# Splitting the last layer's weights: two operations per block on ScalarE and VectorE in place of two on ScalarE and four on GpSimd

## What is computed

```python
x = x + tanh(g_xattn[0]) * fp8_product(layernorm(x), ctx)              # stage A
x = x + tanh(g_ffn[0])   * moe_top2_and_shared(layernorm(x), ...)      # stage B, 8 experts, hidden 128
x = x + tanh(g_xattn[1]) * causal_attention(layernorm(x), ctx, ctx)    # stage C, 16 heads, 4 batches
# stage D, 8 experts, hidden 1024, top 2
probs = softmax(gelu(x @ rw1) @ rw2)
wgt, idx = top_k(probs, 2)
for e in range(8):
    Ye = gelu(x @ w1[e] + b1[e]) @ w2[e] + b2[e]
    ...                                                                # added where idx == e, times wgt
```

## Time and profile before

| | us |
|---|---|
| median of 3 runs | 485.41 |
| lowest, highest | 485.38, 487.7 |
| profiled execution | 489.3 |
| its span, first to last instruction | 487.2 |

### The profile page before, as it was taken

How to read it: one execution, slowest core, us unless ns; L and a number is a source line. 1 busy time by engine, 2 the same in 40 slices (tenths; PEclk the granted TensorE clock), 3 DMA queues, 4 the chain that set the end, 5 groups by cost and what they waited for, 6 DMA issues and landing times.

```text
span 487.2 us, 8683 instructions
## 1 busy us (share of the span) xinstructions
PE 340.7 (70%) x2694; PEld 230.5 (47%) x2695; DVE 316.7 (65%) x787; ACT 269.5 (55%) x541; POOL 182.5 (37%) x232
## 2 busy tenths in 40 slices
PE   0052786977949878468596635008699999999991
PEld 0041324753336565255353312006567777777760
DVE  3978675750554756737779446766757878887870
ACT  1711661054853367858766874614337777777760
POOL 3107026323772414625244554410024455444522
PEclk9996697978979988769979755557989999999997
DMA  8700003604355111463813232365447777777731
GB/s 281 292 0 0 2 0 130 67 0 131 86 147 91 43 49 44 133 108 87 110 45 89 75 111 87 89 217 196 187 146 225 225 227 264 259 223 222 221 34 22
DMA packets 27202, 60.48 MB, mean 124 GB/s; under 512 B 4209, under 2 KB 17858, under 8 KB 23970
## 3 DMA queue, kind: packets, MB, share of 16 engines
q1 hardware_dynamic: 21202, 52.67, 34.8%
q0 software_dynamic: 4416, 6.13, 7.7%
q10 hardware_dynamic: 1552, 1.27, 0.9%
HBM read 29.00 MB, written 6.85 MB: 74 GB/s over the span
## 4 chain that ended last, share of the span: by engine, by line
DVE 23%; PE 22%; issue 18%; ACT 16%; DMA 12%; POOL 5%; ACTq 2%; SPq 1%; DVEq 0%; POOLq 0%
PE bank L1134 9%; ACT arena L1004 5%; DMA STG<-in_l_w_dram 4%; DVE arena L2058 3%; DMA W<-in_ctx_t_dram 3%; ACT arena L1011 3%; POOL W L624 3%; DVE arena L2063 3%; DVE MX L1811 2%; DMA arena<-k_parts 1%; DMA W<-k_parts 1%; DVE arena L2068 1%; ACT STG L791 1%; POOL rstd L599 1%; DMA arena<-token_rows,GI 1%
## 5 line engine op out<-in xcount | busy, mean ns | idle before, releaser
L1467 PE MATMUL bank<-arena 128*128 x184 | 63.4, 390 | 0.9 <-DVE arena L2063 0.9
L1004 ACT ACTIVATE arena<-arena,B1D 128x128 f32<-128x128 f32 x184 | 57.2, 391 | 9.3 <-DVE arena L2058 9.2
L624 POOL TENSOR_TENSOR W<-STG,W 128x256 f16<-128x256 f32 x64 | 41.3, 678 | 50.4 <-ACT W L798 50.4
L2058 DVE TENSOR_REDUCE arena<-bank 128x256 f32<-128x512 f32 x92 | 57.1, 679 | 0.3 <-PE bank L1452 0.3
L691 POOL DMA_INDIRECT arena<-token_rows,GI x23 | 22.9, 995 | 77.3 <-ACT WS L998 56.2
L1470 PE MATMUL bank<-arena 128*128 x184 | 51.2, 278 | 0.0
L1134 PE MATMUL bank<-arena 128*128 128x256 f32 x160 | 44.4, 442 | 7.2 <-ACT arena L839 6.3
L624 POOL TENSOR_TENSOR arena<-STG,arena 128x256 f16<-128x256 f32 x56 | 36.7, 687 | 33.3 <-ACT arena L798 33.3
L704 POOL DMA_INDIRECT out_dram<-arena,SI x23 | 37.0, 1609 | 30.5 <-DMA out_dram<-arena,SI 20.2
L2063 DVE SCALAR_TENSOR_TENSOR arena<-arena 128x512 f16<-128x512 f32 x46 | 29.7, 688 | 26.3 <-ACT arena L1011 25.2
L1449 PE MATMUL bank<-arena 128*128 128x256 f16 x256 | 45.6, 278 | 0.9 <-DVE arena L2010 0.7
(11 more groups left out here) (288 smaller groups left out, 760.0 us busy)
## 6 DMA issues: line engine op xcount, KB each, us to landing
STG<-in_l_w_dram SPq DMA_DIRECT2D x32, 512.0 KB, 3.6
arena<-W SPq DMA_DIRECT2D x16, 1024.0 KB
STG<-W SPq DMA_DIRECT2D x7, 1024.0 KB
arena<-in_l_w_dram SPq DMA_DIRECT2D x2, 1280.0 KB, 11.0
k_parts<-W SPq DMA_DIRECT2D x2, 768.0 KB, 4.9
W<-k_parts SPq DMA_DIRECT2D x12, 128.0 KB, 5.9
arena<-k_parts SPq DMA_DIRECT2D x12, 128.0 KB, 5.8
X<-in_x_dram SPq DMA_DIRECT2D x2, 512.0 KB, 5.7
```

The source lines that it names most:

```text
L624: ins = nc.gpsimd.tensor_tensor(l, src, h, ALU.subtract)
L1004: ins = nc.scalar.activation(x, x, ACT.Gelu, bias=B1D[:, e, c:c + 1], scale=1.0 / (X_SCALE * W_SCALE))
L1467: nc.tensor.matmul(bank[6 + q][:, :], GDL[:, q, 0, c * P:(c + 1) * P], W2[:, e, c].rearrange("p s d -> p (s d)"), start=(c == 0), stop=Fal ...
L2058: v.tensor_reduce(half, o, AX.X, ALU.add).then_inc(s_dadd, 1)
```

## The change

ACT writes the high part straight from the raw block, with the factor 64 in the same operation; the buffer stays raw. DVE computes `64 * raw - high` and writes the low part, in one operation of 1024 columns. POOL does nothing for the weights any more. A block's semaphore chain is load, high (ACT), low (DVE), and load i+2 waits for DVE's low i. The orders written out by hand are new: in stage B DVE's low i follows as `LOW_AFTER` says, in the attention rounds each stands behind every second maximum, and ACT's high i takes one step u where scale and high took two. Loads, and SP's stream as a whole, stand in the order they stood in.

```diff
+        LOW_AFTER = {2 * CA - 8: 3, 2 * CA - 6: 4, 2 * CA - 4: 5, 2 * CA - 2: 6, 2 * CA - 1: 7}
...
             sp.wait_ge(s_eid, 1)
-            sp.wait_ge(s_wlo, BLOCKS - 2)
+            sp.wait_ge(s_wlo, MIDDLE + 2)
             for r in range(2):
                 load_tile_weights(r, r, first=True)
-            sp.wait_ge(s_wlate, 2)
+            sp.wait_ge(s_wlo, BLOCKS)
             load_tile_weights(2, 2, first=True)
...
-                nc.scalar.activation(STG[:, i % 2], STG[:, i % 2], ACT.Copy, scale=W_SCALE).then_inc(s_wscaled, 1)
-
-            def weights_high(i):
-
                 _, hi, _ = weight_block(i)
-                act.wait_ge(s_wscaled, i + 1)
                 src = STG[:, i % 2] if len(hi.shape) == 2 else STG[:, i % 2].rearrange("p (c d) -> p c d", d=D)
-                nc.scalar.activation(hi, src, ACT.Copy).then_inc(s_whi, 1)
+                nc.scalar.activation(hi, src, ACT.Copy, scale=W_SCALE).then_inc(s_whi, 1)
...
+            def weights_low(i):
+
+                _, hi, lo = weight_block(i)
+                dve.wait_ge(s_whi, i + 1)
+                src = STG[:, i % 2] if len(hi.shape) == 2 else STG[:, i % 2].rearrange("p (c d) -> p c d", d=D)
+                v.scalar_tensor_tensor(out=lo, in0=src, scalar=W_SCALE, in1=hi,
+                                       op0=ALU.mult, op1=ALU.subtract).then_inc(s_wlo, 1)
...
                 if b + 1 < B:
+                    blocks = list(C_BLOCKS[b])
                     for u in range(12):
                         maximum(b + 1, u)
+                        if blocks and u % 2:
+                            weights_low(blocks.pop(0))
                     minus_maximum(b + 1)
...
+            for i in D_BLOCKS[3:]:
+                weights_low(i)
+
             def rows_t(j, q, first=False):
```

More of the change, by code:

```diff
@@ L615, in _ @@
             ins.then_inc(s_kparts, 1)
[L617 to L625, removed]
             pool.wait_ge(s_w0, 2)
@@ L649, in _ @@
             pool.wait_ge(s_va, 4)
-            for i in range(9, 11):
-                weights_low(i)
             for g in range(2, 4):
@@ L658, in _ @@
                     estimate_rstd(10, 2, 2)
[L659 to L663, removed]
+                if b == B - 2:
+                    for g in range(2):
+                        estimate_rstd(8 + g, g, 2)
                 if b == 0:
@@ L769, in _, with weights_high @@
             store_xq_t(0, bank[0])
-            def weights_scale(i):
+            def weights_high(i):
                 if i == 0:
@@ L863, in _ @@
             for i in range(3):
-                weights_split(i)
+                weights_high(i)
             store_gates_t(1, bank[2])
@@ L942, in _ @@
             for b in range(B):
-                steps = [(f, i) for i in C_BLOCKS[b] for f in (weights_scale, weights_high)]
+                blocks = list(C_BLOCKS[b])
                 for u in range(12):
@@ L957, in _ @@
                         hidden_weight(b + 1)
-                    if steps and u >= SPLIT_FROM[b]:
-                        f, i = steps.pop(0)
-                        f(i)
+                    if blocks and u >= SPLIT_FROM[b]:
+                        weights_high(blocks.pop(0))
                 store_o(b, 1)
@@ L1775, in _ @@
             choose_gates(1, bank[2])
+            weights_low(0)
             add_down(2)
             store_gate_parts(1, bank[3])
+            weights_low(1)
             add_down(3)
+            weights_low(2)
             dve.wait_ge(s_masks, 4)
@@ L1782, in _ @@
                 gate_hidden(n)
+                if n in LOW_AFTER:
+                    weights_low(LOW_AFTER[n])
                 if n == CA + 3:
@@ L1864, in _ @@
                 maximum(0, u)
+                if u == 6:
+                    weights_low(9)
             minus_maximum(0)
+            weights_low(10)
             add_down(6)
@@ L1896, in _ @@
                     scaled_rows(2)
+                    for i in C_BLOCKS[b]:
+                        weights_low(i)
             for i in range(2):
@@ L1911, in _ @@
                                    op0=ALU.mult, op1=ALU.subtract).then_inc(s_rw, 1)
+            for i in D_BLOCKS[:2]:
+                weights_low(i)
             for h in range(2):
@@ L1924, in _ @@
                             ALU.subtract).then_inc(s_dl, 1)
+            weights_low(D_BLOCKS[2])
             dve.wait_ge(s_ex, 1)
@@ L2024, in _ @@
             v.tensor_tensor(COEF[:, :, 2 * E:3 * E], COEF[:, :, 0:E], SLOTQ[:, :, :], ALU.add).then_inc(s_coef, 1)
-            for i in D_BLOCKS[-2:]:
-                _, hi, lo = weight_block(i)
-                dve.wait_ge(s_whi, i + 1)
-                v.tensor_tensor(lo, STG[:, i % 2].rearrange("p (c d) -> p c d", d=D), hi,
-                                ALU.subtract).then_inc(s_wlate, 1)
             def idle_outputs_out():
```

25 lines of the change are left out of this document (7 added, 18 removed).

## The result

| | before | changed |
|---|---|---|
| median, us | 487.03 (20 runs) | 492.44 (20 runs) |
| ratio of the times, 95% interval | | 1.012 (1.0095 to 1.0145) |
| profiled execution | 489.3 | 491.9 |
| its span | 487.2 | 490.1 |

A forecast was written before the change was run, and what follows sets the result against it. No single engine was taken to bound it: the weight ring, DVE's maxima, key stacks, exponentials, router and first gather did. Terms -3.5 + 1.4 + 1.15 + 0.45 - 3.8 + 9.5 = +5.2 on 485.41 gave 490.6 us, range 484.5 to 496.

The forecast's parts named there:

- Term 1: Second half of stage B: a shorter weight ring starts PE's down(4) earlier, -3.5 us (-4.9 if the fill holds nothing).
- Term 2: Maxima of batch 0: low 9 among them delays the start of round 0, +1.4 us (0 to 1.4).
- Term 3: Attention rounds 0 to 2: DVE's low parts partly in line, less a key stack gain, +1.15 us (-3.2 to +10).
- The key stack's share: Round 0: batch 2's key stack, issued sooner by SP, lets PE start earlier, 3.2 us regained.
- Terms 4 and 5: Round 3, ACT's high 24 waits for its load, +0.45 us; then the way to the router's choice, -3.8 us.
- term 5: Way to the router's choice: DVE's small operations quicker without POOL beside them, router product earlier, -3.8 us (-2.4 to -5).
- Term 6: Token rows: late low 29 holds load 31 and the stores behind it, delaying the first gather, +9.5 us (+6.5 to +11.7).
- about 8 us: Sign of being right: the first gather comes about 8 us behind the row numbers.
- The low bound: Token rows at the start of stage D: +6.5 us if the gather lands sooner with less traffic beside it.
- Rival 2: Token rows not held because the stores go out early: -4.1 us in all, 481.3, chance 0.04.
- Rival 1: Rounds 0 to 2 follow ACT, whose relief gives back 11.6 us while low parts hide: -9.4 in all, 476.0, chance 0.10.
- rival 4: Rounds 0 to 2: every low part in line on DVE, 13.4 us, +9.2 more, 499.8, chance 0.06.

The follow-up runs named there:

- b0: The kernel before, run again with no edit: ratio 0.9984 to the kernel before.
- e3: The kernel before with SP's three token-row stores moved ahead of load 31: ratio 1.0012 to the kernel before.
- a0: The changed kernel, run again with no edit: ratio 1.0133 to the kernel before.
- e1: The changed kernel with DVE's low 29 moved early, right behind the tokens' expert weights: 478.57 us, ratio 0.986 to the kernel before.
- e2: The changed kernel with SP's three token-row stores moved ahead of load 31, DVE's order untouched: 482.08 us, ratio 0.9899 to the kernel before.
- f0: e1 repeated: 479.78 us, ratio 0.9899 to the kernel before.
- f3: f2 with low 9 moved from among batch 0's maxima to behind its negated maximum: 470.67 us, ratio 0.968 to the kernel before.
- e6: The changed kernel with GpSimd's fill held back until DVE's first maximum of batch 0: 493.41 us, ratio 1.0111 to the kernel before.
- e4: The changed kernel with low parts of blocks 11 to 21 (attention rounds 0 to 2) replaced by fp16 copies: ratio 0.9964 to the kernel before.
- e5: The changed kernel with ACT's old two operations for the eleven blocks of rounds 0 to 2: 497.07 us, ratio 1.0198 to the kernel before.
- f1: e1 with the weight work of rounds 0 to 2 (blocks 11 to 21) put back to the old way: 476.69 us, ratio 0.9842 to the kernel before.
- f2: e1 with the first low part of each of rounds 0 to 2 moved into DVE's waits: 473.82 us, ratio 0.9791 to the kernel before.

## Why the prediction was right, term by term

The sum was +5.2 and the time came out at +5.4. That the path was right (a gain ahead of the row numbers, a larger loss behind them) was foresight; that the two figures differ by only 0.2 was in part luck, since the terms below missed by 0.7 to 2 us each, and as measured add up to +2.9. The terms, against the means of the table (three traces of the old order; the changed order's, where a stretch has no further edit):

| term | forecast | measured |
|---|---|---|
| 1, 2: up to max 0 | -2.1 | -3.4 |
| 3: rounds 0 to 2 | +1.15 | +2.3 |
| 4, 5: max 3 to GI | -3.35 | -5.4 |
| 6: GI to the first sums | +9.5 | +10.2 |
| loop | 0 | -0.8 |

**Term 1** was right in mechanism and 0.7 short: down(4) came 4.2 us earlier after the tanh gap, not 3.5, though the fill held DVE as walked. The one difference from the walk that I see is the clock: the first eighteen up products took 4.04 us, not 5.73. The granted clock in their first 4 us was 0.55 to 0.60 in the kernel before and 1.00 in the changed one; b0 and e3 show it lowered there too, and a0, e1, e2, f0 and f3 at 1.00. e6 tested the fill: without the hold down(4) came 1.1 earlier, where I had put 1.4 (4.9 against 3.5). **Term 2**: low 9 was in line, +0.8 from down(4) to max 0; what it may cost through the clock was in no row I had.

**Term 3** had its shape right. Max 0 to 1 grew by 5.6 us (5.4 forecast), max 1 to 2 shrank by 5. Of the 5.6, 1.0 in the mean lies ahead of round 0 (a0, e2 and f0, where the clock fell behind low 9), which I had not priced. The step that failed is how much of a low part reaches the round's end, and what ACT's relief gives: I put a third and nearly nothing; e4 and e5 showed six to nine tenths (8 to 12 us for eleven blocks) and 3 to 8 back. The errors nearly cancelled. The key stack's share was measured by no run alone. SP did issue it sooner, as I had walked, 4.1 to 4.5 us behind max 1 in place of 10.0 to 12.1. But the check I had named, PE waiting less for the keys of batch 2, came out wrong: it waited 5.10 us against 4.62, and 2.5 to 6.0 in the five traces of the changed order against 3.7 to 5.6 in the three of the old. The stretch did shrink, from max 1 to PE's first score 14.3 us against 20.8, but PE reached that point earlier too.

**Terms 4 and 5** were 2 short, nearly all of it in term 5: from max 3 to DVE's first denominator of round 3's output there were 0.2 us less in the mean (+0.45 forecast), from there to GI 5.3 less (-3.8). DVE's four refinement steps took 0.16 each (0.6 in the earlier trace rows), two scalings 0.74 (1.40), the four subtractions behind them 1.43 (2.36, which I had not priced), two comparisons 0.36 (1.27). I had priced three of these four groups.

**Term 6** carried the sign and was right within 1 us. The first gather came 12.1 us behind the row numbers, against 0.9. The sum had it at 335.3 with row numbers at 322.7, 12.6 behind; the "about 8 us" among the signs does not follow from that sum and was wrong. What comes back through low 30 and 31, put at 2.2, is 2.4 by e1 and f0 (10.4 from GI to the sums against 12.8). The sums themselves, named as 5 us later, stood 3.6 later after the tanh gap in the mean of the changed kernel's two traces. The low bound, a gather that lands sooner with less traffic, was the wrong way round: from its issue to DVE's copy 7.7 us passed, not 6.4. In the five traces where it took 7.7 to 8.1 us (changed, a0, e4, e5, e6) SP issued the third load of tile weights (L532) within half a microsecond of it; in e1, f0, f1, f2 and f3, where that load came 5 us behind, 6.2 to 6.4. That is an order of events, not an experiment.

**The rivals.** Rival 2 was excluded by SP's rows. Rival 1 and rival 4 were each half of what happened in the rounds. By the Trainium skill's rule (GPSIMD Engine Reference, section 4.1 Engine selection) elementwise work belongs on VectorE; this case agrees with the factor and shows where the rule stops. Work moved to the faster engine joined a queue in which an unrelated transfer waited three links away. With that undone (e1) the same move is worth 1.0 to 1.4%.

## What to carry to other kernels

When an operation moves to another engine, follow its semaphore to the transfer queue that waits on it, and read what else stands in that queue: one late operation held three stores, a gather and a whole stage here for 11 to 13 us, while the busy times showed 109 us less work on ACT and POOL and 17 more on DVE. Put moved work where the engine waits already (low 16, 19 and 11), never between operations another engine is waiting for. And where two effects of opposite sign meet, test each alone: a right sum says little about its terms.

## What the runs showed of the hardware that I had not expected

- GpSimd's fill of 3.51 us, which only writes, held a tensor_scalar of 128x2 for 3.41 to 3.51 us in all ten traces in which they met. Reductions of PSUM ran at full speed beside it (e6). The tensor_tensor operations of the same size just ahead took 0.15 and 0.16, but they had ended within 0.1 us of the fill's start, so no run shows what it does to them. I had priced it as holding whatever stands beside it. The Trainium skill states this difference (SBUF — State Buffer, section Who interferes with whom): a VectorE instruction with two SBUF inputs contends with a GpSimd instruction that reads SBUF, not with one that only writes; tensor_scalar can enter a mode that contends; a reduction never does on this chip. The traces agree on the tensor_scalar and on the reductions.
- A low part that began beside a GpSimd tensor_tensor took 1.52 us in place of 1.22 (low 16 in f2), and DVE's 128x2 steps, 0.6 in the earlier trace rows, take 0.16 or 0.17 with GpSimd idle. By the same section, two inputs in SBUF contend with GpSimd's reads; the rows agree for the low part and for the three of the four steps that have two inputs.
- An fp16 copy of 1024 columns within SBUF took 0.42 us on DVE, a third of the 1.22 of the operation with two inputs.
